# GCN stage of a kernel of four graph networks: neighbour sums before the projection, with the adjacency as the streamed operand

## The reference, cut to what matters

```python
def _normalize_adjacency(adj):
    adj_self = adj + jnp.eye(N)
    d_inv_sqrt = adj_self.sum(axis=2) ** (-0.5)
    return adj_self * d_inv_sqrt[:, :, None] * d_inv_sqrt[:, None, :]

h = jnp.maximum(_layernorm(x, axis=-1), 0.0)
x = x + L0(h, adj); ...                      # attention network
x = x + L1(h, adj, nodemask); ...            # three message layers and a final projection of their outputs
h = jnp.maximum(_layernorm(x, axis=-1), 0.0)
support = jnp.einsum('bni,io->bno', h, L2_gnn_weight)
x = x + jnp.einsum('bnm,bmo->bno', adj_norm, support) + L2_gnn_bias    # the GCN stage
h = jnp.maximum(_layernorm(x, axis=-1), 0.0)
x = x + relu(((adj > 0).T @ h) @ U / deg)                               # last network
```

## Time and profile before

| what | us |
| --- | --- |
| median of three runs | 1330.38 |
| profiled execution, its own time | 1330.83 |
| its span in the trace | 1329.1 |
| GCN stage: first real work on TensorE to the first matmul of the next phase | 1052.2 to 1221.0 |
| neighbour sums: first matmul to last | 1067.3 to 1217.4 |

### The profile page before, as it was taken

How to read it: one execution, slowest core, us unless ns; L and a number is a source line. 1 busy time by engine, 2 the same in 40 slices (tenths; PEclk the granted TensorE clock), 3 DMA queues, 4 the chain that set the end, 5 groups by cost and what they waited for, 6 DMA issues and landing times. The chain is left out here.

```text
span 1329.1 us, 29132 instructions
## 1 busy us (share of the span) xinstructions
PE 1204.1 (91%) x10849; PEld 1033.7 (78%) x10849; DVE 791.4 (60%) x2835; ACT 595.4 (45%) x1519; POOL 114.8 (9%) x129
## 2 busy tenths in 40 slices
PE   4999799988598999998989999899998899998998
PEld 4999666655377787777869999799998599996554
DVE  5999455566655655565542544444536466676983
ACT  4888246766644454454322333404343432332441
POOL 4432000000000000000000000023323010110000
PEclk9999889987599999999989999999999899999999
DMA  9977011111235665446324756036757335462931
GB/s 323 314 262 278 2 23 27 28 19 22 73 155 222 229 248 200 183 191 244 126 89 174 301 219 274 1 120 246 282 211 285 127 127 207 186 241 84 407 96 48
DMA packets 105523, 229.06 MB, mean 172 GB/s; under 512 B 34529, under 2 KB 53153, under 8 KB 105377
## 3 DMA queue, kind: packets, MB, share of 16 engines
q1 hardware_dynamic: 104656, 227.07, 46.3%
q10 hardware_dynamic: 720, 0.07, 0.0%
HBM read 185.70 MB, written 37.75 MB: 168 GB/s over the span
## 5 line engine op out<-in xcount | busy, mean ns | idle before, releaser
L1371 PE MATMUL lay_acc<-lay_z,k_otheradj 128*128 128x128 f32 x1024 | 118.3, 277 | 0.0
L1371 PEld LDWEIGHTS lay_acc<-lay_z,k_otheradj 128*128 128x128 f32 x1024 | 117.1, 194 | 0.0
L1371 PE MATMUL lay_acc<-lay_z,k_keepadj 128*128 128x128 f32 x1024 | 117.0, 275 | 0.0
L1371 PEld LDWEIGHTS lay_acc<-lay_z,k_keepadj 128*128 128x128 f32 x1024 | 115.6, 192 | 0.0
L1419 ACT ACTIVATE lay_junk<-lay_o 128x128 bf16<-128x128 f32 x128 | 37.7, 295 | 124.2 <-DVEq L1508 123.9
L1102 ACT ACTIVATE fuse_dist<-fuse_prank,k_kb 128x512 f16<-128x512 f32 (+2 forms) x96 | 55.2, 575 | 76.1 <-PE fuse_prank L993 72.9
L1485 DVE TENSOR_TENSOR lay_o<-lay_ring,k_vec 128x512 f32<-128x512 f32 x32 | 22.1, 692 | 106.2 <-PE lay_ring L1364 106.2
L1465 POOL TENSOR_TENSOR lay_bl<-k_vec,k_mask 128x256 f32<-128x256 f32 x32 | 21.2, 664 | 617.9 <-DVEq L1498 614.2
L993 PE MATMUL fuse_prank<-k_fore,k_T 128*128 128x128 fp8e5 (+3 forms) x416 | 63.3, 291 | 10.5 <-PEq L140 7.2
L333 PE MATMUL att_acc<-att_rhs,att_adjT 128*128 128x130 f32 x512 | 59.8, 280 | 13.9 <-POOLq L285 12.3
L333 PEld LDWEIGHTS att_acc<-att_rhs,att_adjT 128*128 128x128 f32 x512 | 59.1, 195 | 14.4 <-POOLq L285 12.4
(11 more groups left out here) (288 smaller groups left out, 2722.4 us busy)
## 6 DMA issues: line engine op xcount, KB each, us to landing
k_keepadj<-in_adj_cols SPq DMA_DIRECT2D x28, 1024.0 KB, 9.1
k_keepadj<-keptT SPq DMA_DIRECT2D x12, 2048.0 KB, 10.8
k_otheradj<-keptT SPq DMA_DIRECT2D x12, 2048.0 KB, 11.5
att_adjT<-in_adj_cols SPq DMA_DIRECT2D x16, 1024.0 KB, 8.2
k_otheradj<-in_adj_cols SPq DMA_DIRECT2D x16, 1024.0 KB, 10.5
keptT<-k_keepadj SPq DMA_DIRECT2D x16, 1024.0 KB, 4.6
keptT<-k_otheradj SPq DMA_DIRECT2D x16, 1024.0 KB, 4.3
lay_rowf<-in_adj_rows SPq DMA_DIRECT2D x32, 512.0 KB, 14.6
```

The costliest lines, as they stand in the source:

```text
L1371: mm = t.matmul(acc[i % 2][k][:, ib % HB, :], adjT[i % 2][:, jb, ib * P:(ib + 1) * P], zz[i % 2][:, jb, :], start=(jb == 0), stop=(jb == N ...
```

## The change

- `sup`, `turn`, `turned_copy` and `support` go. ScalarE's `normalise` now writes D h into one of two buffers `hs`, since `scales` multiplies the layer norm's scale by D with one small instruction more on VectorE (two for each graph).
- `sums(b, hf)` now loads a tile of `hs` (128 rows x 128 features) as weights and streams 512 columns of the adjacency past it, 8 matmuls for each half hf of the columns. The result is the sums transposed, features x rows, in `agg`.
- ScalarE's `turned_sums` copies it to `aggT`, and `project(b, hf)` multiplies it with `W2`, four matmuls for each half. `project(b, 1)` comes after `sums(b+1, 0)`.
- The self loop is now part of the adjacency: `self_loops(b)` on VectorE waits for the graph's adjacency, adds the identity to its eight diagonal tiles and releases `loop_added`, for which `sums(b, 0)` waits.
- `finish` multiplies the projected sums by D from PSUM and adds them to x; its first instruction is gone.
- The jump parts are made two graphs ahead (`jump`), with a wait for the reader of their PSUM buffer (`jump_read`).
- `degrees` comes before the first `normalise`. At the end, ScalarE's norm of graph 0 for the next phase comes behind both `turned_sums` of graph 7, and the parts (`next_parts`) behind `finish(7, 0)`.

The diff, cut to its core:

```diff
--- TensorE
-                def sums(b, ibs):
-                    for ib in ibs:
-                        for jb in range(NB):
-                            mm = t.matmul(acc[ib // HB][:, ib % HB, :], adjT[b % 2][:, jb, ib * P:(ib + 1) * P],
-                                          sup[b % 2][:, jb, :], start=(jb == 0), stop=(jb == NB - 1))
+                def sums(b, hf):
+                    sl = slice(hf * HALF, (hf + 1) * HALF)
+                    for jb in range(NB):
+                        if hf == 0 and jb % HB == 0:
+                            pe.wait_ge(h_ready, 2 * b + jb // HB + 1)
+                        mm = t.matmul(agg[b % 2][:, sl], hs[b % 2][:, jb, :], adjT[b % 2][:, jb, sl], start=(jb == 0), stop=(jb == NB - 1))
+                    mm.then_inc(agg_ready, 1)
+                def project(b, hf):
+                    pe.wait_ge(aggT_ready, 2 * b + hf + 1)
+                    if b > 0:
+                        pe.wait_ge(pr_read, 2 * (b - 1) + hf + 1)
+                    for ib in range(hf * HB, (hf + 1) * HB):
+                        mm = t.matmul(pr[1][:, ib, :], aggT[:, ib * P:(ib + 1) * P], K["W2"][:], start=True, stop=True)
+                    mm.then_inc(pr_ready, 1)
+                keep_busy(t, K, agg[0][:, 0:HALF], 12)
+                jump(0)
+                keep_busy(t, K, agg[1][:, 0:HALF], 22)
+                jump(1)
                 for b in range(B):
+                    pe.wait_ge(loop_added, b + 1)
+                    sums(b, 0)
                     if b > 0:
+                        project(b - 1, 1)
+                    if b + 2 < B:
+                        jump(b + 2)
+                    sums(b, 1)
                     pe.drain().then_inc(adj_used, 1)
+                    project(b, 0)
+                project(B - 1, 1)
--- ScalarE
+                        if b >= 2:
+                            act.wait_ge(agg_ready, 2 * (b - 2) + 2)
                         for t in range(half * HB, (half + 1) * HB):
+                            last = a.activation(hs[b % 2][:, t, :], K["X"][:, b * NB + t, :], ACT.Relu, ...)
                 for b in range(B):
+                    if b + 2 < B:
+                        entry(b + 2)
+                    if b + 1 < B:
+                        normalise(b + 1)
+                    turned_sums(b, 0)
+                    turned_sums(b, 1)
                 norm_root(nc, act, K, w, 2 * B)
+                norm_apply(nc, act, lambda t: K["X"][:, t, :], K["h"][:], w, 2 * B, h_ready)
--- VectorE
+                def self_loops(b):
+                    adjacency_there(dve, b)
+                    for jb in range(NB):
+                        own = adjT[b % 2][:, jb, jb * P:(jb + 1) * P]
+                        last = v.tensor_tensor(own, own, K["ident"][:], ALU.add)
+                    last.then_inc(loop_added, 1)
@@ scales
+                    v.tensor_tensor(s_[:, 1, ts], s_[:, 1, ts], dinv[:, b * NB + half * HB:b * NB + (half + 1) * HB], ALU.mult)
+                    dve.drain()
@@ finish
-                    v.tensor_tensor(y[:], acc[k][:], sup[b % 2][:, of_half(k), :], ALU.add)
-                    dve.drain().then_inc(sums_read, 1)
-                    v.tensor_tensor(y[:], y[:], along_features(dinv[:, cols], D), ALU.mult)
+                    v.tensor_tensor(y[:], pr[1][:, of_half(k), :], along_features(dinv[:, cols], D), ALU.mult)
+                    dve.drain().then_inc(pr_read, 1)
@@ order
+                degrees()
                 normalise(0)
-                degrees()
-                support(0)
+                self_loops(0)
                 for b in range(B):
                     if b + 1 < B:
                         normalise(b + 1)
-                    else:
+                    if b > 0:
+                        finish(b - 1, 1)
+                    if b + 1 == B:
                         norm_mean(nc, dve, tiles(K["X"], 0, NB), w)
                         norm_scale(nc, dve, w, 2 * B)
+                    if b + 1 < B:
+                        self_loops(b + 1)
                     finish(b, 0)
                     if b + 1 == B:
                         next_parts()
-                    finish(b, 1)
-                    if b + 1 < B:
-                        support(b + 1)
+                finish(B - 1, 1)
```

More of the change, by code:

```diff
@@ L1593, in of_half, with adjacency_there @@
             return slice(half * HB, (half + 1) * HB)
-        def projected(b, k, half):
-            return 4 * b + 2 * k + half + 1
+        def adjacency_there(engine, b):
+            if b < 2:
+                engine.wait_ge(first_loaded[b], 32)
+            else:
+                engine.wait_ge(loaded[b % 2], 32 * (b // 2))
         with nc.Block() as block:
@@ L1610, in _, with jump @@
                 t = nc.tensor
[L1612 to L1619, removed]
+                def jump(b):
                     for half in range(2):
-                        pe.wait_ge(hT_ready if k else eT_ready, 2 * b + half + 1)
+                        pe.wait_ge(eT_ready, 2 * b + half + 1)
+                        if b > 0:
+                            pe.wait_ge(jump_read, 2 * (b - 1) + half + 1)
@@ L1637, in _ @@
[L1637 to L1642, removed]
-                for b in range(B):
-                    if b + 1 < B:
[L1645 to L1650, removed]
-                    if b > 0:
[L1652 to L1660, removed]
+                            mm = t.matmul(pr[0][:, ib, :], eT[:, ib * P:(ib + 1) * P], K["Wl"][:, 2, :], start=True, stop=True)
@@ L1675, in entry @@
                         else:
-                            act.wait_ge(pr_ready, projected(b - 1, 0, half))
+                            act.wait_ge(jump_ready, 2 * (b - 1) + half + 1)
                         sl = slice(half * HALF, (half + 1) * HALF)
@@ L1691, in normalise, with turned_sums @@
                         last.then_inc(h_ready, 1)
[L1693 to L1697, removed]
+                def turned_sums(b, hf):
+                    act.wait_ge(agg_ready, 2 * b + hf + 1)
+                    if b > 0:
+                        act.wait_ge(pr_ready, 2 * (b - 1) + hf + 1)
+                    sl = slice(hf * HALF, (hf + 1) * HALF)
+                    a.activation(aggT[:, sl], agg[b % 2][:, sl], ACT.Copy).then_inc(aggT_ready, 1)
@@ L1723, in _ @@
                 v = nc.vector
+                def self_loops(b):
[4 more added lines that the diff above has]
+                    last.then_inc(loop_added, 1)
                 def update(b, half):
-                    dve.wait_ge(pr_ready, projected(b, 0, half))
+                    dve.wait_ge(jump_ready, 2 * b + half + 1)
                     for ib in range(half * HB, (half + 1) * HB):
@@ L1771, in degrees @@
                     dve.drain()
-                def support(b):
-                    for half in range(2):
-                        dve.wait_ge(pr_ready, projected(b, 1, half))
-                        ts = of_half(half)
-                        v.tensor_tensor(sup[b % 2][:, ts, :], pr[1][:, ts, :],
-                                        along_features(dinv[:, b * NB + half * HB:b * NB + (half + 1) * HB], D), ALU.mult)
-                        dve.drain().then_inc(sup_ready, 1)
                 def finish(b, k):
-                    dve.wait_ge(sums_ready, 2 * b + k + 1)
+                    dve.wait_ge(pr_ready, 2 * b + k + 1)
                     cols = slice(b * NB + HB * k, b * NB + HB * (k + 1))
                     xs = K["X"][:, cols, :]
-                    v.tensor_tensor(y[:], acc[k][:], sup[b % 2][:, of_half(k), :], ALU.add)
-                    dve.drain().then_inc(sums_read, 1)
-                    v.tensor_tensor(y[:], y[:], along_features(dinv[:, cols], D), ALU.mult)
-                    dve.drain()
+                    v.tensor_tensor(y[:], pr[1][:, of_half(k), :], along_features(dinv[:, cols], D), ALU.mult)
+                    dve.drain().then_inc(pr_read, 1)
                     if k == 0:
```

43 lines of the change are left out of this document (14 added, 29 removed).

## The result

The changed kernel takes 1319.68 us in the median of four runs (1319.07 to 1321.43), the kernel before 1330.14 on the same occasion (four runs, 1329.29 to 1331.5). The ratio is 0.9923, 95% interval 0.9905 to 0.994: 10.5 us less. The forecast was 1321.4, between 1313 and 1330, and faster.

What follows compares the result with a forecast made beforehand. The prediction held the stage bound by TensorE's instruction list. Head -5.0, clock +1.5, list -14.1 and tail +8.2 summed to -9.4 us, taking the profiled 1330.83 to 1321.4, with a range of 1313 to 1330 for 8 in 10.

Steps and rivals of the forecast that it cites:

- clock behind the idle stretch: Head: TensorE idles 1.6 us, then runs some 3 us at the lower clock within the first sums; cost 1.5 us.
- The price that decides: Sums: a float32 instruction of 512 columns costs 0.43 us, twice bf16's 0.216, between bounds of 0.216 and 0.447.
- the step of narrow matmuls: Sums before: 128-column steps of 0.110 (bf16) and 0.112 us (float32) might mean float32 columns cost no more.
- FP32_LOW_HIGH: Sums: the skill's halved TensorE rate, read for each instruction 0.43 us, for a whole float32 matmul 0.216.
- The list: First to last sum: TensorE's instructions take 17.7 us a graph against 19.4, 136.0 in all against 150.1; gain 14.1.
- Who could be late: Between graphs: load and self loops finish about 2 us before TensorE needs them; the other engines' work stays hidden.
- My count of TensorE's steps: From a buffer's release: projections, sums and a 1.8 us jump; the graph using the new adjacency starts 18.6 us later.
- The head: Stage start: without transposes and projection ahead, sums start at 1062.3 instead of 1067.27; gain 5.0 us.
- The tail: Stage end: norm and parts for the next phase come after the last sum, 10.5 us against 2.3; cost 8.2.
- Streaming at 0.216: Sums: 512 float32 columns cost one bf16 price, the load's ring then binds; some 1294 us, chance 0.05.
- Rival 4: Between graphs: self loops end 3 us late on VectorE, seven times, TensorE waits; 1342 us, chance 0.08.
- Its collision: Self loops: GpSimd's bias addition falls on VectorE's additions and holds them up, 2.4 us.

Runs made afterwards that it cites:

- narrow: Changed kernel with the sums made as before, 128 columns streamed, 64 matmuls a graph instead of 16 of 512: 1325.62 us, ratio 0.996 to the kernel before.
- Loops4: Changed kernel with 24 more additions into an unread tile ahead of each graph's eight self loops: 1347.08 us, ratio 1.0118 to the kernel before.
- tail2: Changed kernel with the next phase's norm and parts moved ahead of graph 6's last finish (VectorE) and graph 7's copies (ScalarE): 1313.87 us, ratio 0.9871.
- best: tail2 with the self loops of graph 0 also moved ahead of its norm on VectorE: 1311.84 us, ratio 0.9853 to the kernel before.
- best_warm: best with 16 matmuls whose result nobody reads added behind the last projection: 1314.62 us, ratio 0.9873 to the kernel before.
- cold: Changed kernel with 12 instead of 22 unread matmuls between the two jumps, lengthening TensorE's idle stretch before the first sums: 1322.71 us, ratio 0.9936.

## Why the prediction was right, point by point

| term | forecast | measured |
| --- | --- | --- |
| a sum instruction of 512 columns | 0.43 us | 0.429 |
| first sum, from its old place | -5.0 | -4.9 |
| clock behind the idle stretch | +1.5 | +0.1 |
| first to last sum, without the clock | 136.0 (-14.1) | 136.6 (-13.6) |
| last sum to the end | +8.2 | +8.2 |
| sum | -9.4 | -10.3 |

- **The price that decides.** The durations of the nearest rows, which double with float32, gave the right value, and the step of narrow matmuls did not mislead. Of the two readings of the Trainium skill's FP32_LOW_HIGH (Perfetto Trace Analysis, Engine Utilization), the one for each instruction agrees with this trace, if the name means the float32 of this kernel: 0.429 against 0.216.
- **The list.** Of the 13.6 us, 4.5 are the width (shown by narrow). The seven sets of transposes that lay between the first and last sum, 0.87 us each, account for 6.1 by the rows of before; no run puts them back alone. The other 3 us are what remains. The waits of the weight loads for the projected rows, 3.3 us in seven times, fit it in size; that is argued and not shown by a run. The list was 0.6 us longer than forecast, 17.80 a graph instead of 17.7.
- **Who could be late.** The self loops took 1.71 us for 1.8 forecast. Their slack was 2.9 to 3.4 us in graphs 2 to 6, where I had about 2. Two things went otherwise. My count of TensorE's steps has a jump part of 1.8 us in every graph, and graph 6 has none: by the same count graph 7 is left 0.5 us (16.8 for 16.3), not 2. It had 1.6: its additions ended 15.6 us behind the issue of its load (1166.56), and TensorE asked at 17.2. And I had GpSimd's bias addition end before the load lands. In graph 3 the load landed 12.9 us behind its issue (1108.24 for 1095.34) and met it:

```profile
1106.96 2.34 POOL L1714 TENSOR_TENSOR k_X<-k_X,k_vec 128x1024 f32<-128x1024 f32 x1 [15.46 <-ACT gcn_hs L1683]
...
1108.24 2.62 DVE L1726 TENSOR_TENSOR k_otheradj<-k_otheradj,k_ident 128x128 f32<-128x128 f32 x8 [1.63 <-DMA k_otheradj<-in_adj_cols]
```

  The longest single addition took 1205 ns. Graphs 5 and 7 met it too, with 2.42 and 2.05 us. It was covered in all three.
- **The head.** 1062.3 was forecast, 1061.80 measured, with a stage that began 0.54 us earlier. The last self loop was just ahead of the bias addition (1061.75 and 1061.89), as hoped.
- **The failed term** is the clock, +1.5, of which 0.1 came. I had read one case, 1.67 us idle, as a rule for 1.6. The idle stretch was 1.49 us, and the clock held. With that term at 0.1 the sum is -10.8 for -10.3 measured: the list, 0.5 us short of its forecast gain, hid a third of the clock's error, and that is luck. Of the 1.7 us between the forecast of 1321.4 and the measured 1319.68, 0.9 lie in the terms and 0.7 in the base, 1330.83 where the occasion's median was 1330.14.
- **The tail** came out to a tenth, since each of its steps had a row in before.
- **The rivals.** Streaming at 0.216 did not happen, nor any wait for self loops behind graph 0. Loops4 shows how the slower side would have come: additions 5.3 us longer make the kernel 1.2% slower than before. Rival 4 multiplied its wait by seven, but only six graphs load within the stage. Its collision was real, in three graphs.

## What to carry to other kernels

When a change shortens the list of the engine that binds, price the steps at both ends of the stage as well: here the middle gave 13.5 us, and a preparation that lost its cover at the end took 8.2 back, until it was moved (and it moved in full only when what was queued ahead of it was looked at). Which operand is streamed decides how many instructions a product takes, and for float32 a wide one gains only some 4%; what follows from the choice, here that no transposes are needed, can be worth more. Before trusting a new wait to slack, add work in front of it until it shows, and look for the round in which a step is missing from the binding engine's list: the slack is smallest there.

## What the runs showed of the hardware

- A float32 matmul is two instructions here. They follow each other every 0.112 us with 128 columns and every 0.429 us with 512; the weight loads of 192 ns lie beside the matmul before.
- The granted clock behind an idle stretch of TensorE: after 0.66, 1.15, 1.35 and 1.49 us it stayed at 1.00 in every case of this stage and its end; after 1.67 (before), 2.52, 3.13, 3.65 and 8.96 us it fell to 0.50, and the work behind ran longer by up to 3.0 us. Yet 1.81 us ahead of the last graph's sums in the kernel before cost nothing (128 instructions in 14.56 us, the usual step). At the start of the last network it fell after 3.52 us in the kernel before and after 3.44 in tail2, and stayed after 3.44 in best; and an idle stretch of 1.94 us was followed by 0.53 of the clock in best_warm (from 1219.60 to 1222.00), one of 1.93 us by 1.00 in best. Length alone doesn't decide; what else does stays open. A wait can cost nearly twice its length: 3.65 us and 3.0 more in cold.
- VectorE's additions of two SBUF operands stood still while GpSimd's addition ran: a 128x128 addition took 1205 ns at most in place of 280, and ended 0.15 us behind GpSimd's (1109.30). The Trainium skill (SBUF — State Buffer, SBUF: two separate sides) calls it an exclusive lock, and the trace agrees.
